# A third bank for layer 0's turned blocks, earlier mix copies and norm at the expert handover, an own bank for batch 1's logits

## The chip, the cores and the metric

The kernel runs on one core of a Trainium2 chip. The metric is the device time of one execution in microseconds (us), as a median of several runs. Beside it one execution was taken with the hardware profiler; all times of single instructions come from that one.

## The reference, cut to what matters

Two layers, each a gated cross attention and a gated feed-forward, on x of 2 batches x 256 tokens x 128:

```python
x = x + tanh(g_xattn[0]) * xattn0(layernorm(x), ctx, ctx)   # 16 heads of 8, ctx 2 x 512 x 128, mask
x = x + tanh(g_ffn[0])   * ffn0(layernorm(x))               # Hadamard, 4 bit activations, ternary weight
x = x + tanh(g_xattn[1]) * xattn1(layernorm(x), ctx, ctx)   # 16 heads of 64, mask per batch
x = x + tanh(g_ffn[1])   * moe(layernorm(x))
# attention: scores = q k / sqrt(d); softmax over 512 keys; out = probs v; out @ Wo.T + bo
# moe: softmax of 32 logits, the 4 largest with a capacity per expert, silu(x W1) * (x W3) @ W2,
#      all 32 experts of 64, summed with the gates, plus one shared expert of 128
```

## The kernel before

**Units and blocks.** An attention is cut into units: one head (layer 1) or one head of 8 (layer 0) with 128 queries against 512 keys. 64 units are layer 0's, 64 layer 1's (`TOTAL` = 128). Eight units in layer 0, four in layer 1, make a `Block` (0 to 7, and 8 to 15). Every engine runs the same written-out order of slots t from -6 on, and waits on semaphores alone.

**A unit's way.** TensorE computes scores (`scores`, L1299, in slot t for unit t+6, two score banks). VectorE masks them and takes the maximum (`mask_max`, L913, unit t+5), ScalarE takes the exponential (L729, unit t+4; it waits until the turn of six units before has freed the row buffer), VectorE the reciprocal of the sum (L922, t+3), GpSimd normalises (L586, t+3). TensorE turns the 128 x 512 block with four transposes (`turn`, L1323, unit t) into one of two `turn_bank` (banks 2 and 3), and VectorE (even units) or ScalarE (odd units and some listed ones) copies it to `probsT` (`copy_turned`, L929 and L737) in slot t+1. The turn of unit u waits for the copy of unit u-2.

**A block's end.** `mix` (L1329) multiplies all turned blocks with the values, in slot end+2 in layer 0 and end+3 in layer 1, the very last in end+1. Within a slot TensorE goes scores, jobs, mix, output projection, turn. ScalarE copies the mix (`mix_copy`, L741) in slot `copy_at`, and TensorE projects out (`project_out`, L1352) in slot `out_at` into `y_bank` (bank 7), in layer 0 once per batch. `Block` sets these slots (L81 to L83).

**Jobs.** Projections, layer norms' transposes, values and the small matmuls of feed-forward and router are "jobs" (`make_plan`, L115), placed by hand in slots and alternating over two `job_banks` (banks 5 and 6); a job waits for its bank's release by the job before it there. DMAs go through SP's queue, in the plan's order.

**Handover to the experts.** From slot 127 (`EXPERTS_AT`) the expert phase runs in halves n = 0 to 33 (17 for each batch; half p of batch b). A step e has two halves: TensorE computes `up` for W1 (even p) and W3 (odd p, six matmuls each), then `down` of the step three before. ScalarE does silu (L857), VectorE `multiply` (L1149) and `hidden` (L1162, with the gates that SP loads by DMA), ScalarE the high half of hidden (`high_hid`, L837), GpSimd its low half (`low_hid`, L630). The hidden of batch 1's steps (9, 10, ...) need batch 1's gates. In the halves of batch 0 stand still: the last attention slots (`attend(127 + p)`), layer 1's add, norm and router of batch 1 (`LATE_JOBS` L107 and `LATE_ROUTER` L108 give the halves), and weight splits on GpSimd (`WEIGHTS_LATER`, L166). Batch 1's last norm is turned, its logits computed, their maximum and exponentials taken, four experts selected, ranked, and the gates turned (`turn_gate`), written by DMA and loaded again. All these late jobs share bank 6. ScalarE takes a late job one half after TensorE, ahead of that half's silu.

## Time and profile before

| | |
|---|---|
| median of 3 runs | 278.34 us (277.91 to 278.48) |
| profiled execution | 278.08 us, its span 276.3 us |
| busy: TensorE / VectorE / ScalarE / GpSimd | 254.2 / 211.6 / 190.9 / 181.0 us |
| mean granted TensorE clock | 0.994 |
| layer 0's slots | about 16 to 90 us, its last turns to 103 us |
| layer 1's slots | to about 225 us |
| experts | 225.6 to 274 us |

A busy share is a mean over stages; the stretches and single waits in them say more. The idle time that a row gives in brackets is that of the row's engine just before it, with what released it.

### The profile page before, as it was taken

What the parts mean: (1) busy time and instruction counts of PE and PEld (TensorE: products, weight loads), DVE (VectorE), ACT (ScalarE), POOL (GpSimd) and SP (SyncE); (2) the same over time, 40 slices, a digit from 0 to 9 for tenths busy, and PEclk for the clock granted to TensorE, in tenths of its full rate; (3) what the DMA queues carried; (4) which work ended last, traced back from release to release, by engine and by line L of the source; (5) the groups of instructions that cost most, each with busy time, mean ns of one, the idle gap of its engine ahead of it and who ended that gap; (6) DMA issues with size and microseconds to landing.
All of it is one profiled execution on the core that took longest, in us unless ns stands there. A gap on an engine that the chain in (4) does not pass through costs nothing. (4 is left out here: it accounts for less than half of the span.)

```text
span 276.3 us, 6695 instructions
## 1 busy us (share of the span) xinstructions
PE 254.2 (92%) x1903; PEld 201.0 (73%) x1903; DVE 211.6 (77%) x654; ACT 190.9 (69%) x454; POOL 181.0 (65%) x271
## 2 busy tenths in 40 slices
PE   7897999999778998989999999999979989799994
PEld 5565766676547786778777788877757767799993
DVE  3999889889959795889677877787797524685683
ACT  3488779888769785857776776776866563656462
POOL 7367999675888675745743685348757794916380
PEclk9999999999999999999999999999999999889999
DMA  6558375100023675635484767676441131301540
GB/s 197 213 165 283 130 266 140 54 2 4 1 66 71 133 153 117 135 88 121 118 217 114 185 165 180 175 180 174 120 97 34 51 108 38 105 13 36 181 115 19
DMA packets 25987, 32.91 MB, mean 119 GB/s; under 512 B 4000, under 2 KB 18144, under 8 KB 25824
## 3 DMA queue, kind: packets, MB, share of 16 engines
q1 hardware_dynamic: 25520, 32.27, 43.5%
q8 instruction: 16, 0.26, 0.4%
q10 hardware_dynamic: 432, 0.22, 0.3%
q14 instruction: 19, 0.16, 0.2%
HBM read 14.32 MB, written 3.47 MB: 64 GB/s over the span
## 5 line engine op out<-in xcount | busy, mean ns | idle before, releaser
L586 POOL TENSOR_SCALAR probs<-probs,rsum 128x512 f32<-128x512 f32 x128 | 87.9, 693 | 59.0 <-DVE rsum L922 58.3
L729 ACT ACTIVATE probs<-masked,neg_max 128x512 f32<-128x512 f32 x128 | 91.8, 718 | 12.7 <-DVE neg_max L913 9.1
L1196 PE MATMUL bank<-ident,probs 128*128 128x128 f32 x512 | 78.5, 276 | 4.0 <-DVE probsT L929 2.5
L1196 PEld LDWEIGHTS bank<-ident,probs 128*128 128x128 f32 x512 | 58.5, 141 | 21.2 <-issue 11.2
L913 DVE CUSTOM_DVE_ANT_0 masked<-bank,mask 128x512 f32<-128x512 f32 x64 | 43.8, 684 | 16.4 <-PE bank L1321 16.0
L737 ACT ACTIVATE probsT<-bank 128x512 f32<-128x512 f32 x74 | 43.4, 587 | 16.5 <-PE bank L1196 16.5
L1348 PE MATMUL bank<-probsT,val 128*32 128x256 f32 (+1 forms) x512 | 46.6, 384 | 0.9 <-ACT mixT L747 0.9
L929 DVE COPY probsT<-bank 128x512 f32<-128x512 f32 x54 | 36.7, 680 | 12.5 <-PE bank L1196 12.3
L913 DVE CUSTOM_DVE_ANT_0 masked<-bank,shared 128x512 f32<-128x512 f32 x64 | 43.3, 676 | 0.4 <-PE bank L1314 0.3
L1348 PEld LDWEIGHTS bank<-probsT,val 128*32 128x32 f32 (+1 forms) x512 | 24.7, 123 | 19.0 <-issue 5.9
L1314 PE MATMUL bank<-parts 128*128 128x512 f32 x64 | 31.3, 489 | 4.4 <-DVE neg_max L913 4.4
L1320 PE MATMUL bank<-k_high,q 128*128 128x512 f32 x64 | 30.5, 477 | 1.4 <-DMA q<-q_split 1.1
L630 POOL TENSOR_TENSOR q<-masked,q 128x512 fp32r<-128x512 f32 (+1 forms) x16 | 19.9, 1258 | 17.0 <-ACT q L837 16.9
L1321 PE MATMUL bank<-k_both,q 128*128 128x512 f32 x64 | 25.2, 394 | 0.0
L729 ACT ACTIVATION_READ_ACCUMULATOR probs<-masked,neg_max 128x1 f32 x128 | 24.6, 192 | 0.0
L1149 DVE TENSOR_TENSOR bank<-bank,probsT 128x512 f32<-128x512 f32 x16 | 11.1, 696 | 13.2 <-PE bank L1203 11.6
L922 DVE RECIPROCAL rsum<-sums 128x1 f32<-128x1 f32 x128 | 20.0, 157 | 0.7 <-ACT probs L729 0.7
L857 ACT ACTIVATE probsT<-bank 128x512 f32<-128x512 f32 (+1 forms) x18 | 10.3, 572 | 14.6 <-PE bank L1203 10.4
L1314 PEld LDWEIGHTS bank<-parts 128*128 128x128 f32 x64 | 12.0, 188 | 9.3 <-DVE neg_max L913 6.7
L777 ACT ACTIVATE k_high<-bank,cols 128x512 fp32r<-128x512 f32 x16 | 11.0, 689 | 8.8 <-PE bank L1203 8.8
L986 DVE SCALAR_TENSOR_TENSOR k_low<-bank,cols,k_high 128x512 fp32r<-128x512 f32 x16 | 12.0, 748 | 6.3 <-ACT k_high L777 6.3
L837 ACT ACTIVATE q<-masked 128x512 fp32r<-128x512 f32 (+1 forms) x18 | 10.7, 603 | 4.3 <-DVE masked L1162 3.3
(238 smaller groups left out, 526.9 us busy)
## 6 DMA issues: line engine op xcount, KB each, us to landing
k_both<-k_low SPq DMA_DIRECT2D x32, 128.0 KB, 2.9
k_both<-k_high SPq DMA_DIRECT2D x32, 128.0 KB, 2.8
q<-q_split SPq DMA_DIRECT2D x32, 128.0 KB, 2.4
probsT<-staged_gate SPq DMA_DIRECT2D x32, 128.0 KB, 2.9
q<-q_split SPq DMA_DIRECT2D x32, 64.0 KB, 2.0
parts<-staged_k SPq DMA_DIRECT2D x7, 256.0 KB, 2.7
w_flat<-in_w SPq DMA_DIRECT2D x1, 1536.0 KB, 7.8
staged_k<-k_high SPq DMA_DIRECT2D x2, 512.0 KB, 3.1
```

What stands on the lines that cost most here:

```text
L586: pool.tensor_scalar(p, p, rsum[:, u % NCOL:u % NCOL + 1], 1.0, ALU.mult, ALU.mult).then_inc(normed, 1)
L630: pool.tensor_tensor(hid_low[:, e % RING, 0:cols], hidT[:, e % RING, 0:cols], hid_high[:, e % RING, 0:cols].bitcast(F32), ALU.subtract).th ...
L729: act.activation(probs[:, u % NP, :], masked[:, u % NS, :], ACT.Exp, scale=-1.0, bias=neg_max[:, c:c + 1], accum_out=sums[:, c:c + 1]).the ...
L737: act.activation(probsT[:, k.m % 2, h, :, qt * P:qt * P + P], turn_bank[u % 2][:, :].rearrange("p (k q) -> p k q", q=P), ACT.Copy).then_in ...
L913: dve.tensor_tensor_reduce(out=masked[:, u % NS, :], in0=score_bank[u % 2][:, :], in1=mask, scale=-float(k.depth) ** -0.5, scalar=3.0e38, ...
L922: dve.reciprocal(rsum[:, c:c + 1], sums[:, c:c + 1]).then_inc(recipped, 1)
L929: dve.tensor_copy(probsT[:, k.m % 2, h, :, qt * P:qt * P + P], turn_bank[u % 2][:, :].rearrange("p (k q) -> p k q", q=P)).then_inc(copied[ ...
L1196: ins = pe.transpose(dst[0:rows, t * P:t * P + P], src, ident[:, :])
L1314: pe.matmul(dst, q0[:, k.m % 4, h, q], k0[:, k.m % 4, :], start=True, stop=True).then_inc(scored, 1)
L1320: pe.matmul(dst, q1_high[:, s, h, q], k1_high[:, s, :], start=True, stop=False)
L1321: pe.matmul(dst, q1_both[:, s, h, q], k1_both[:, s, h, :], start=False, stop=True).then_inc(scored, 1)
L1348: ins = pe.matmul(mix_bank[w * h:w * h + w, 0:SQ], v[:, i, w * h:w * h + w], probsT[:, k.m % 2, h, i, :], start=(first and i == 0), stop=( ...
```

## The change

Four things are changed. (1) Layer 0's turned blocks go round three banks: 2, 3 and 7, with semaphores `copied0`; a turn waits for the copy three units back. Bank 7 was the output projection's, so layer 0's projection becomes a job `out` in a job bank, in the same slot. Layer 1 keeps two banks; its first two turns wait for layer 0's last copies in their banks. (2) The last two blocks' mix copies and projections are one slot earlier, and ScalarE takes the last attention slots two at a time, ahead of the silu. (3) Batch 1's last add, statistics and norm are one half earlier; GpSimd takes its rstd ahead of two weight splits; ScalarE and VectorE take the norm's turned block in the half in which it is turned. (4) Batch 1's logits get bank 7 and wait for ScalarE's copy of the norm only; rank and turned gates move one half later (13 to 14, 15 to 16), the router's last step two (13 to 15).

```diff
-        self.copy_at = self.mix_at + (2 if layer == 1 and not last else 1)
-        self.out_at = self.copy_at + 1
+        late = layer == 1 and b == B - 1 and g >= self.groups - 2
+        self.copy_at = self.mix_at + (2 if layer == 1 and not late else 1)
+        self.out_at = self.copy_at + (0 if last else 1)
...
-LATE_JOBS = {"ln": 7, "logits": 8, "rank": 13, "turn_gate": 15}
-LATE_ROUTER = {4: (0, 1), 6: (3,), 9: (6,), 10: (8, 9, 10), 13: (12,)}
+LATE_JOBS = {"ln": 7, "logits": 8, "rank": 14, "turn_gate": 16}
+LATE_ROUTER = {3: (0, 1), 5: (3,), 9: (6,), 10: (8, 9, 10), 15: (12,)}
...
+    for k in (BLOCKS[3], BLOCKS[7]):
+        plan.setdefault(k.out_at, []).append(("out", k.b))
...
-        i = 1 if j in last else number[j] % 2
+        i = 2 if j == ("logits", 1) else 1 if j in last else number[j] % 2
...
+def turn_home(u):
+
+    return u % 3 if u < L1_AT else u % 2
+
+
+def copies_before(i, u):
+
+    return (u - i + 2) // 3
...
-        job_banks = bank[5:7]
+        turn_bank0 = [bank[2], bank[3], bank[7]]
+        job_banks = bank[5:8]
...
             for e in range(2 * STEPS):
+                if e == 1:
+                    rstd_of(3, 1)
                 for n in WEIGHTS_LATER.get(e, ()):
                     split_weights(n)
-                if e == 1:
-                    rstd_of(3, 1)
                 low_hid(e)
...
-                    if b == 0:
+                    if b == 0 and p % 2 == 0:
+
                         attend(EXPERTS_AT + p)
+                        attend(EXPERTS_AT + p + 1)
                     for j in AFTER.get(n - 1, ()):
-                        job(j)
+                        if j != ("ln", 3, 1):
+                            job(j)
                     if p % 2 == 0:
                         wide = 2 * SQ if p < PAIRS else SQ
                         act.wait_ge(u_ready, e + 1)
                         if e >= 2:
                             act.wait_ge(hid_ready, e - 1)
                         act.activation(silu[:, e % 2, 0:wide], u_bank[e % 2][:, 0:wide], ACT.Silu).then_inc(silu_ready, 1)
+                        if n + 1 == LATE_JOBS["ln"]:
+                            job(("ln", 3, 1))
...
-                    for j in AFTER.get(n - 1, ()):
-                        job(j)
+                    for j in AFTER.get(n, ()) + AFTER.get(n - 1, ()):
+                        if (j in AFTER.get(n, ())) == (j == ("ln", 3, 1)):
+                            job(j)
...
+                elif name == "out":
+                    pe.wait_ge(mix_copied, j[1] + 1)
+                    for t in range(NQ):
+                        ins = pe.matmul(job_bank[:, t * P:t * P + P], mixT[:, (j[1] + 1) % 2, t * P:t * P + P], w0T[:, 3, :],
+                                        start=True, stop=True)
...
                 elif name == "logits":
                     pe.wait_ge(ld["wg"], 16)
-                    pe.wait_ge(*freed(("ln", 3, j[1])))
+                    pe.wait_ge(half_done, 2 * j[1] + 1)
+                    if j[1]:
+                        pe.wait_ge(y_used, 2)
...
             def turn(u):
                 pe.wait_ge(normed, u + 1)
-                if u >= 2:
-                    pe.wait_ge(copied[u % 2], u // 2)
-                turn_tiles(turn_bank[u % 2], [probs[:, u % NP, i * P:i * P + P] for i in range(NK)]).then_inc(turned, 1)
+                i = turn_home(u)
+                if u < L1_AT:
+                    if u >= 3:
+                        pe.wait_ge(copied0[i], u // 3)
+                elif u < L1_AT + 2:
+                    pe.wait_ge(copied0[i], copies_before(i, L1_AT))
+                else:
+                    pe.wait_ge(copied[i], (u - L1_AT) // 2)
...
-                for i in range(2):
-                    pe.wait_ge(copied[i], k.end // 2)
+                if k.layer:
+                    for i in range(2):
+                        pe.wait_ge(copied[i], (k.end - L1_AT) // 2)
+                else:
+                    for i in range(3):
+                        pe.wait_ge(copied0[i], copies_before(i, k.end))
```

## Rows read from the trace of the kernel before

**Rows 1.** Windows: us, then busy us (instructions) of PE, PEld, DVE, ACT, POOL, PEclk, DMA

```profile
10.00:90.00 80.00, 70.54 (x551) 50.20 (x551) 71.54 (x255) 65.52 (x167) 62.45 (x97) 1.00 0.37 116
90.00:218.00 128.00, 124.22 (x921) 98.71 (x922) 100.90 (x313) 91.47 (x225) 78.87 (x123) 1.00 0.56 136
...
240.00:244.00 4.00, 4.00 (x23) 4.00 (x23) 2.06 (x7) 3.41 (x7) 1.60 (x2) 0.58 0.25 66
244.00:268.00 24.00, 24.00 (x207) 23.66 (x206) 17.41 (x36) 13.10 (x26) 13.35 (x11) 1.00 0.33 96
```

**Rows 2.** Waits from 10 to 90 us: us in total, times, longest

```profile
DVE probsT L929 <- PE bank L1196: 5.8, 5, 1.6
...
PE bank L1196 <- DVE probsT L929: 2.5, 9, 0.6
```

**Rows 3.** Timeline, DVE and PE around one mix: start, us, engine, line

```profile
46.46 0.67 DVE L913 CUSTOM_DVE_ANT_0 masked<-bank,shared 128x512 f32<-128x512 f32 x1
...
47.21 0.48 PE L1314 MATMUL bank<-parts 128*128 128x512 f32 x1
...
47.62 1.94 PE L1348 MATMUL bank<-probsT,val 128*32 128x256 f32 x32
...
50.18 0.69 DVE L929 COPY probsT<-bank 128x512 f32<-128x512 f32 x1 [1.03 <-PE bank L1196]
```

**Rows 4.** Timeline, PE and ACT between layer 0 and layer 1

```profile
89.92 0.63 PE L1196 MATMUL bank<-ident,probs 128*128 128x128 f32 x4 [0.36 <-ACT probsT L737]
...
101.42 0.58 ACT L737 ACTIVATE probsT<-bank 128x512 f32<-128x512 f32 x1
...
101.55 0.60 PE L1196 MATMUL bank<-ident,probs 128*128 128x128 f32 x4
...
104.54 0.47 PE L1320 MATMUL bank<-k_high,q 128*128 128x512 f32 x1 [1.13 <-DMA q<-q_split]
```

**Rows 5.** Timeline, ACT, PE and DVE at the handover to the experts

```profile
223.31 1.95 PE L1348 MATMUL bank<-probsT,val 128*64 128x256 f32 x16
...
227.56 0.48 ACT L747 ACTIVATE mixT<-bank,cols 128x256 f32<-128x256 f32 x1
...
228.19 1.95 PE L1348 MATMUL bank<-probsT,val 128*64 128x256 f32 x16 [0.93 <-ACT mixT L747]
...
232.61 0.71 PE L1361 MATMUL bank<-w_out,mixT 128*128 128x128 f32 x4 [0.41 <-ACT mixT L747]
...
233.65 0.48 DVE L902 SCALAR_TENSOR_TENSOR x_sb<-bank,tanh_g,x_sb 128x256 f32<-128x256 f32 x1
...
237.97 0.41 PE L1196 MATMUL bank<-ident,xn 128*128 128x128 f32 x2 [1.09 <-DVE xn L893]
...
239.69 0.77 PE L1283 MATMUL bank<-wg,xnT 128*128 128x32 f32 x4 [0.60 <-DVE x_low L959]
```

**Rows 6.** Timeline, DVE, ACT and POOL in batch 1's logits and selection

```profile
240.49 0.23 DVE L1072 TENSOR_REDUCE lg<-bank 128x2 f32<-128x64 f32 x1 [0.95 <-PE bank L1283]
...
242.54 0.20 ACT L801 ACTIVATION_READ_ACCUMULATOR small<-bank,lg 128x1 f32 x1
...
243.40 0.16 DVE L1077 RECIPROCAL lr<-ls 128x2 f32<-128x2 f32 x1
...
245.26 1.29 POOL L630 TENSOR_TENSOR q<-masked,q 128x512 fp32r<-128x512 f32 x1 [3.66 <-ACT q L837]
...
245.40 1.23 DVE L1090 TENSOR_TENSOR small<-small,room 128x64 f32<-128x64 f32 x1
...
247.18 0.19 DVE L1093 CAST sel_b<-small 128x64 bf16<-128x64 f32 x1
```

**Rows 7.** Timeline, ACT and DVE from the turned gates to their first use

```profile
251.11 0.36 ACT L805 ACTIVATE xq<-bank 32x256 f32<-32x256 f32 x1
...
251.96 0.63 ACT L837 ACTIVATE q<-masked 128x512 fp32r<-128x512 f32 x1 [0.23 <-DVE masked L1162]
...
257.12 0.69 DVE L1162 TENSOR_TENSOR masked<-bank,probsT 128x512 f32<-128x512 f32 x1 [0.90 <-DMA probsT<-staged_gate]
```

More of the change, by code:

```diff
@@ L144, in make_plan @@
     last = [j for o in after for j in after[o]]
-    place, count = {}, [0, 0]
+    place, count = {}, [0, 0, 0]
     for j in order:
-        i = 1 if j in last else number[j] % 2
+        i = 2 if j == ("logits", 1) else 1 if j in last else number[j] % 2
         place[j] = (i, count[i])
@@ L154, in make_plan @@
             highs[j] = count
+    after = {o: tuple(js) for o, js in after.items()}
     return before, plan, after, number, place, highs
@@ L370, in build @@
         copied = [sem("copied0"), sem("copied1")]
+        copied0 = [sem(f"copied0_{i}") for i in range(3)]
         mixed = sem("mixed")
@@ L736, in copy_turned @@
                     act.wait_ge(mixed, k.m - 1)
+                i = turn_home(u)
                 act.activation(probsT[:, k.m % 2, h, :, qt * P:qt * P + P],
-                               turn_bank[u % 2][:, :].rearrange("p (k q) -> p k q", q=P),
-                               ACT.Copy).then_inc(copied[u % 2], 1)
+                               (turn_bank if k.layer else turn_bank0)[i][:, :].rearrange("p (k q) -> p k q", q=P),
+                               ACT.Copy).then_inc((copied if k.layer else copied0)[i], 1)
             def mix_copy(k):
@@ L743, in mix_copy @@
                 act.wait_ge(mixed, k.m + 1)
-                if n >= 3:
-                    act.wait_ge(projected_out, n - 2)
+                if n in (3, 4):
+                    act.wait_ge(job_done, NUMBER["out", n - 3] + 1)
+                elif n > 4:
+                    act.wait_ge(projected_out, n - 4)
                 bias = bv1[:, k.g:k.g + 1] if k.layer else bv0[:, 0:1]
@@ L751, in job @@
                 name, n = j[0], NUMBER[j]
-                if name in ("v0", "v1", "ffn", "rank", "rotate"):
+                if name in ("v0", "v1", "ffn", "rank", "rotate", "out"):
                     return
@@ L898, in add_y @@
                 x = x_sb[:, NQ * b:NQ * b + NQ, :]
-                y = (moe_bank[0][:, 0:SQ] if layer == 2 else y_bank[:, b * SQ:b * SQ + SQ]).rearrange("p (t c) -> p t c", c=P)
+                y = (job_banks[PLACE["out", b][0]][:, 0:SQ] if layer == 0 else moe_bank[0][:, 0:SQ] if layer == 2
+                     else y_bank[:, b * SQ:b * SQ + SQ]).rearrange("p (t c) -> p t c", c=P)
+                used, n = freed(("out", b)) if layer == 0 else (y_used, 2 * layer + b - 1)
                 if layer < 2:
@@ L902, in add_y @@
                 dve.scalar_tensor_tensor(out=x, in0=y, scalar=tanh_g[:, gate:gate + 1], in1=x,
-                                         op0=ALU.mult, op1=ALU.add).then_inc(y_used, 1)
-                dve.wait_ge(y_used, 2 * layer + b + 1)
+                                         op0=ALU.mult, op1=ALU.add).then_inc(used, 1)
+                dve.wait_ge(used, n)
             def mask_max(u):
@@ L928, in copy_turned @@
                     dve.wait_ge(mixed, k.m - 1)
+                i = turn_home(u)
                 dve.tensor_copy(probsT[:, k.m % 2, h, :, qt * P:qt * P + P],
-                                turn_bank[u % 2][:, :].rearrange("p (k q) -> p k q", q=P)).then_inc(copied[u % 2], 1)
+                                (turn_bank if k.layer else turn_bank0)[i][:, :]
+                                .rearrange("p (k q) -> p k q", q=P)).then_inc((copied if k.layer else copied0)[i], 1)
             def job(j):
@@ L1039, in feed_forward @@
                 if o == 0:
-                    dve.wait_ge(projected_out, b + 1)
+                    dve.wait_ge(job_done, NUMBER["out", b] + 1)
                     dve.wait_ge(tanh_ready, 1)
@@ L1324, in turn @@
                 pe.wait_ge(normed, u + 1)
-                if u >= 2:
-                    pe.wait_ge(copied[u % 2], u // 2)
-                turn_tiles(turn_bank[u % 2], [probs[:, u % NP, i * P:i * P + P] for i in range(NK)]).then_inc(turned, 1)
-            def mix(k):
-                for i in range(2):
-                    pe.wait_ge(copied[i], k.end // 2)
+                i = turn_home(u)
+                if u < L1_AT:
[5 more added lines that the diff above has]
+                    pe.wait_ge(copied[i], (u - L1_AT) // 2)
+                turn_tiles((turn_bank0 if u < L1_AT else turn_bank)[i], [probs[:, u % NP, n * P:n * P + P] for n in range(NK)]).then_inc(turned, 1)
+            def mix(k):
+                if k.layer:
[4 more added lines that the diff above has]
+                        pe.wait_ge(copied0[i], copies_before(i, k.end))
                 if k.layer == 0:
@@ L1354, in project_out @@
                 pe.wait_ge(mix_copied, n)
-                if k.layer == 1 and k.g == 0:
+                if k.g == 0:
                     pe.wait_ge(ld["bo1"], 32)
-                if (k.layer == 0 or k.g == 0) and (k.layer or k.b):
-                    pe.wait_ge(y_used, 2 * k.layer + k.b)
+                    if k.b:
+                        pe.wait_ge(y_used, 1)
+                    else:
+                        pe.wait_ge(copied0[2], copies_before(2, L1_AT))
                 for t in range(NQ):
@@ L1361, in project_out @@
                     ins = pe.matmul(y_bank[:, c:c + P], mixT[:, n % 2, t * P:t * P + P],
-                                    w1_out[:, k.g, :] if k.layer else w0T[:, 3, :],
-                                    start=((k.layer == 0 or k.g == 0) and t == 0),
+                                    w1_out[:, k.g, :], start=(k.g == 0 and t == 0),
                                     stop=(k.g == k.groups - 1), skip_group_check=True)
@@ L1387, in attend @@
                         mix(k)
-                    if t == k.out_at and (k.layer or k.g == 3):
+                    if t == k.out_at and k.layer:
                         project_out(k)
@@ L1417, in down @@
                 if d == 0 and b:
-                    pe.wait_ge(y_used, 4)
+                    pe.wait_ge(*freed(("logits", 1)))
                 if b == 0:
```

17 lines of the change are left out of this document (9 added, 8 removed).

## The prediction

> **What bounds the kernel now.** I read the windows first, then the waits in each, then the order of single instructions at the waits. Three stretches have three limits. In layer 0 (10 to 90 us) VectorE is busy 71.5 of 80 us; in layer 1 (90 to 218 us) TensorE is busy 124 of 128 us; from 244 to 268 us TensorE has no gap, 207 matmuls in 24.00 us, so 0.116 us each [rows 1]. In the matmul-bound stretches a gain is passed on to the end and nothing of it is lost; between layer 1 and the last stretch stand the gaps of the handover, with a clock at 0.58 from 240 to 244 us [rows 1]. So two places can pay: VectorE's stalls in layer 0, and the handover.
>
> **Third bank for layer 0's turned blocks.** What it takes away is TensorE's wait for the copy two units back. That wait is 2.5 us in nine places, but VectorE, the bound, waits for turned blocks only 5.8 us in five places [rows 2]. Is it the same wait? [rows 3] show one of the five. VectorE ends the masking of unit E+6 at 47.13 (46.46 plus 0.67); the scores of unit E+8, which need its score bank, start at 47.21; the mix of 32 matmuls follows at 47.62 and takes 1.94, and the turn is behind it; the copy waits for that turn until 50.18, 1.03 us. No copy is late there: TensorE is held by the two score banks and by the mix's own 1.9 us, and both stay. So the third bank is worth nothing at the mixes. Where it does count is where ScalarE or VectorE has a job in front of a copy and TensorE reaches something that VectorE needs: in the trace at 89.92, where the turn waits 0.36 us for ScalarE's copy and the first layer 1 scores stand behind it [rows 4]. I take 0.3 us for that. Bounds: nothing, and 0.8 us (0.36 and the other late turns, of 0.3 us each, if one more of them counts).
>
> Against it stand three costs. Unit 64 turns into the bank that unit 63 left, so its turn now waits for copy 63, which ScalarE starts at 101.42 and ends at 102.0 [rows 4]. The turn ran at 101.55, so it and the scores, query job and turn queued behind it move by 0.5 us. The scores of unit 72 wait 1.13 us for the queries' DMA until 104.54 [rows 4]; the DMAs in question were issued before, so the 0.5 us is covered, and shows in full if that DMA comes a microsecond earlier. The output projection as a job keeps its matmuls and its slot, at equal cost; it holds a job bank until VectorE's add one slot on, while the next job that depends on it, `turn_x`, waits for that add anyway: nothing, bound 0.3 us. Mixes wait for three semaphores, not two, eight times: nothing, bound 0.1 us each or 0.8 us in all. Layer 0 and its end together: **-0.3 us**, between -0.8 and +0.8.
>
> **Last mixes' copies.** ScalarE takes both copies of the last two blocks ahead of its silus. Now mixT of block 14 is copied at 227.56, behind silu 0 and copy 127, and the last mix starts at 228.19 after 0.93 us of waiting; the last output projection waits 0.41 us at 232.61 [rows 5]. The mix of block 14 starts at 223.31 and ends after 1.95, at 225.3 [rows 5]; the first silu's matmuls come only after it, so ScalarE can copy it before. Block 15's copy stands before silu 1, whose matmuls come after the mix anyway. What hides its 0.48 us is the six matmuls (0.7 us) between. Both waits go: -1.3 us on TensorE.
>
> **Norm in front.** VectorE adds the output projection and takes statistics in half 3, before hidden 1, and normalises in half 5, not 6; GpSimd computes rstd before two weight splits. Added waits: VectorE stands at the add until projection 15 ends, with multiply 1 behind it, whose matmuls come right after that projection, so nothing is held. The turn of the norm waits 1.09 us at 237.97 now [rows 5]. On the new order xn is there at about 235.0, by my estimate: the mix starts at 227.5 behind projection 14, so projection 15 ends at 230.8, 2.8 us before the add of now at 233.65 [rows 5]; add 0.5 us and statistics 0.9, multiply and hidden 1 at 0.69 each [rows 7], the two normalisations 1.4, with GpSimd beside them. TensorE arrives at the same time, so this wait goes too. The turn is then up to 2.9 us earlier: 0.93, 0.41, 1.09, and 0.4 us of other time around such waits.
>
> **Own bank for the logits.** They wait for ScalarE's copy alone, and no longer for VectorE's low half: the 0.60 us at 239.69 go [rows 5]. Summed, TensorE waits 3.0 us less (0.93 + 0.41 + 1.09 + 0.60). The half-speed clock, which set in after these waits, costs 4.00 x (1 - 0.58) = 1.7 us [rows 1] and I expect it to go with them. TensorE alone would gain 4.7 us.
>
> **Which wait ends last then.** Not TensorE's. Batch 1's gates come at the end of a chain: maximum of the logits, exponentials, selection, rank, turned gates, DMA out and back, and hidden 9. That one already waited for DMA until 257.12 [rows 7], some 0.1 us from holding TensorE. So I follow the chain.
> - Maximum: before it VectorE has two multiply and hidden pairs and the low half, 2 x 1.4 + 0.4 us, from 235.0: 238.3, where it was 240.49 [rows 6]: 2.2 us earlier.
> - Exponentials: from the end of the maximum (240.72) to their last read (242.74) 2.0 us, table load within; the selection started at 243.40, since VectorE was still in hidden 4 [rows 6]. Now hidden 4 is done first: ScalarE, 0.2 us late from its own high half, ends at 240.8. So 2.6 us earlier.
> - Selection: 3.9 us to the cast's end at 247.3. In it one comparison took 1.23 us; it stood from 245.40 to 246.6 beside a GpSimd subtraction from 245.26 to 246.55, and the two operations of its size between it and the cast at 247.18 fill 0.55 us together [rows 6]. So 1.0 us of the chain is that meeting, and whether it happens again depends on where GpSimd's low half of step 4 falls: by the same counting 243.2, in the midst of the last operations. I take half: 3.1 us earlier, between 2.6 and 3.6.
> - Turned gates: the job moves from half 15 to 16, so on ScalarE it goes behind the high half of step 7, not 6. That copy ran at 251.96 to 252.6, the job at 251.11 [rows 7]. So the move costs 1.5 us: 1.6 us earlier, between 1.1 and 2.1.
> - DMA: from the turned gates at 251.11 to hidden 9 at 257.12 are 6.0 us [rows 7]. That tail moves as a whole; SP has nothing else in front.
>
> TensorE comes 3.4 us earlier (4.7 less 0.5 at the rank, which it reaches a little before the selection is done, and 0.8 where down 5 waits for GpSimd) and waits at steps 12 and 13 for hidden 9 and 10. Then it is busy to the end. The end thus moves by the chain: **-1.6 us**.
>
> **Sum.** Profiled execution: 278.08 - 0.3 - 1.6 = 276.2 us. The median of the runs was 278.34, 0.26 above that execution, so 276.4 us. The forecast's own range is 275.4 to 277.6: the low end takes both bounds, the high one the larger of them alone, since the two have nothing in common.
>
> The Trainium skill (SBUF — State Buffer, Who interferes with whom) has the two engines share a port pair, and the later of a two-input VectorE instruction and a reading GpSimd instruction blocks until the first ends; the pair at 245.26 and 245.40 agrees. By that rule each of the selection's operations with two inputs can meet a low half, and two meetings instead of half a one would leave the chain 0.1 us early instead of 1.6.
>
> **Rivals.**
> - *Gates are not last* (0.10). If the chain is as fast as TensorE, because ScalarE's job finds its place sooner, the end moves by TensorE's 3.4 to 4.1 us, with the first 0.3: 274.3. For it: hidden 9's wait was only 0.90 us. Against: the job order on ScalarE is fixed.
> - *The clock falls again* (0.11). TensorE gets new waits, 0.9 us at down 5 and 0.8 to 1.0 us at steps 12 and 13, in front of the stretch that has no slack. A fall like that at 240 costs 1.7 us: 278.1. Against: two gaps, of 1.09 and 0.60 us [rows 5], stood just before that one, while TensorE's wait of 1.13 us at 104.54 [rows 4] left the clock at 1.00 [rows 1].
> - *Selection meets GpSimd twice, or the third bank costs its bound* (0.07): 278.34 - 0.3 - 0.1, or 278.34 + 0.8 - 1.6, 277.7 in the middle.
> - *The mixes' stall goes as well* (0.07). Should the turn bank be what holds TensorE there after all, 5.8 us of VectorE's stalls go, with 1.6 at the end: 271.
> - *Slower: the late turn_gate* (0.11). The chain gains only by its start; its two jobs were moved back. If the maximum isn't earlier, as GpSimd or the rstd holds the norm behind low half 0, the 1.5 us of the later place are all that is left: 278.34 + 1.5 - 0.3 = 279.5. It decides as soon as the selection starts less than 1.5 us earlier than at 243.40. The same holds if the change doesn't do what it says at the norm.
>
> **Chances.** Forecast 0.54, the rivals as given. A measurement here tells about 0.2%, 0.56 us. Faster by more than that: 0.54 + 0.10 + 0.07 and a third of the rival of 277.7, 0.73; within it the rest of that one and the clock, 0.15; slower 0.12. The range for 8 in 10 takes in the gates and the clock rival and leaves out the two outer ones: 274.2 to 278.2.
>
> **What the profile after should show.** In 10 to 90 us VectorE's waits for turned blocks still 5 to 6 us, with TensorE's for copies nearly gone; a turn near 101 waiting for ScalarE's copy. No wait at the last mix, projection, norm turn and logits; clock 1.00 at 240 us; selection from about 240.5; the turned gates' copy near 249.2; hidden 9 waiting over 2 us for DMA, and TensorE waiting at steps 12 and 13. Wrong would be: stalls at the mixes of other length, a clock fall behind 245, or a gates' copy later than 250.5.

## The result, and the profile after

The changed kernel took 279.81 us (median of 6 runs, 279.02 to 280.81) beside 278.29 us for the kernel before (6 runs): a ratio of 1.0051, 95% interval 1.0030 to 1.0073. In a second comparison it was 279.19 against 278.15 us, 1.0038 (1.0020 to 1.0055). So it is 1.0 to 1.5 us slower, where 276.4 was forecast and 274.2 to 278.2 was the range. Its profiled execution took 279.41 us with a span of 276.5 (before: 278.08 and 276.3).

The windows of the changed kernel, with the columns of [rows 1], and its waits from 10 to 90 us and from 218 to 277 us:

```profile
10.00:90.00 80.00, 69.46 (x555) 50.73 (x553) 71.55 (x252) 65.52 (x167) 62.57 (x97) 1.00 0.38 116
90.00:218.00 128.00, 124.66 (x921) 98.68 (x920) 101.42 (x315) 91.93 (x225) 79.39 (x123) 1.00 0.56 136
240.00:244.00 4.00, 3.96 (x30) 3.61 (x30) 2.63 (x13) 3.84 (x9) 1.61 (x2) 1.00 0.20 63
244.00:268.00 24.00, 20.12 (x169) 19.55 (x170) 15.66 (x26) 11.12 (x22) 12.64 (x11) 1.00 0.34 96
```

```profile
PE bank L1351 <- DVE neg_max L940: 8.9, 17, 1.3
...
DVE probsT L957 <- PE bank L1226: 5.8, 5, 1.6
...
DVE masked L1191 <- DMA probsT<-staged_gate: 3.1, 1, 3.1
...
PE bank L1231 <- DVE masked L1191: 1.8, 2, 1.5
```

Read against [rows 1 and 2]: VectorE's five waits for turned blocks in layer 0 are still 5.8 us. TensorE no longer waits for copies there but for VectorE's maxima, 8.9 us in place of these:

```profile
PE bank L1314 <- DVE neg_max L913: 4.4, 7, 1.2
```

The half-speed clock at 240 us is gone in this trace. And the stretch that had no gap, 244 to 268 us, now has 3.9 us of idle TensorE. It came early and waited 1.23 us for the selection and 0.86 for ScalarE's high half, and then 1.50 and 0.33 us for VectorE, which waited 3.1 us for the gate rows:

```profile
245.19 0.20 PE L1328 MATMUL bank<-sel_b,ones_b 128*128 128x32 bf16 x2 [1.23 <-DVE sel_b L1122]
...
257.98 0.38 PE L1231 MATMUL bank<-x_high,w_early 128*128 128x256 f32 x1 [1.50 <-DVE masked L1191]
```

The steps between layer 0 and layer 1, and the handover (TensorE and ScalarE; compare [rows 4 and 5]):

```profile
102.01 0.63 PE L1226 MATMUL bank<-ident,probs 128*128 128x128 f32 x4 [0.46 <-ACT probsT L755]
104.07 0.47 PE L1357 MATMUL bank<-k_high,q 128*128 128x512 f32 x1 [0.17 <-DVE neg_max L940]
...
225.14 0.47 ACT L767 ACTIVATE mixT<-bank,cols 128x256 f32<-128x256 f32 x1 [0.66 <-PE bank L1395]
...
227.47 1.95 PE L1395 MATMUL bank<-probsT,val 128*64 128x256 f32 x16
230.16 0.61 PE L1410 MATMUL bank<-w_out,mixT 128*128 128x128 f32 x4
235.38 0.41 PE L1226 MATMUL bank<-ident,xn 128*128 128x128 f32 x2 [0.37 <-DVE xn L918]
236.34 0.57 PE L1320 MATMUL bank<-wg,xnT 128*128 128x32 f32 x4
```

Every step of the handover is earlier than in [rows 5]: the norm's turn by 2.59 us (237.97 to 235.38), the logits by 3.35 (239.69 to 236.34). The chain of the gates goes on from there (compare [rows 6 and 7]):

```profile
238.25 0.21 DVE L1101 TENSOR_REDUCE lg<-bank 128x2 f32<-128x64 f32 x1
...
241.06 0.17 DVE L1106 RECIPROCAL lr<-ls 128x2 f32<-128x2 f32 x1 [1.21 <-ACT small L821]
...
243.59 1.23 DVE L1121 TENSOR_TENSOR small<-small 128x64 f32<-128x64 f32 x1
244.85 0.20 DVE L1122 CAST sel_b<-small 128x64 bf16<-128x64 f32 x1
...
249.36 0.38 PE L1226 MATMUL bank<-ident,small 128*32 128x128 f32 x2
...
249.97 0.63 ACT L857 ACTIVATE q<-masked 128x512 fp32r<-128x512 f32 x1 [1.20 <-DVE masked L1191]
250.50 0.36 ACT L825 ACTIVATE xq<-bank 32x256 f32<-32x256 f32 x1
...
257.23 0.69 DVE L1191 TENSOR_TENSOR masked<-bank,probsT 128x512 f32<-128x512 f32 x1 [3.13 <-DMA probsT<-staged_gate]
```

| step of the gates' chain | before | after | earlier by |
|---|---|---|---|
| maximum of the logits | 240.49 | 238.25 | 2.24 |
| selection starts | 243.40 | 241.06 | 2.34 |
| selection's cast | 247.18 | 244.85 | 2.33 |
| copy of the turned gates | 251.11 | 250.50 | 0.61 |
| tenth product (hidden 9) | 257.12 | 257.23 | -0.11 |

So the gain of 2.3 us is lost in two places: 1.7 us between cast and copy, where the two jobs were moved one half later, and 0.7 us in the transfer behind the copy, whose length had been 6.01 and is 6.73 us. From the tenth product to the end both kernels run alike (VectorE's last add at 273.57 and 273.70).

**The transfer behind the copy.** The turned gates are stored to DRAM and read back as rows. A landing is one increment of the transfer's semaphore; one issue has 16 of them, and the reader waits for the last. SP issues the loads of a step's gate rows in two halves. The loads' time from issue to landing (least, median, most, in us), first of the kernel before for its first two (issued at 253.0 and 253.6), then of the changed kernel (252.4 and 253.0):

```profile
DMA to landing us min/median/max: 2.8/3.1/3.4
```

```profile
DMA to landing us min/median/max: 2.8/3.5/4.1
```

The first half takes as long as before, the second 0.7 us longer. The view of the DMA queues of the changed kernel from 254.8 to 255.0 us (queue, kind, packets, MB, share of 16 engines' time) shows what else ran:

```profile
q1 hardware_dynamic: 35, 0.03, 57.2%
q8 instruction: 1, 0.02, 29.2%
```

One packet of 16 KB on queue 8, of the kind "instruction", started at 254.90 and took 0.93 us. Before, such a packet came at 257.40, after the rows had landed (257.00). There are 16 or 17 of them in a run, about one for each 256 instructions of TensorE's stream (4285 before, 4292 after; nearly all come 180 to 260 instructions behind a multiple of 256, by a count of TensorE's instructions in the traces). So I take them for loads of TensorE's program: where TensorE is in its program sets when they come. "Load" below means such a packet. The change made TensorE 2.5 us earlier there and the gates only 0.6, and the packet slid from behind the rows into them. The rows' two loads land in 32 parts: 31 of them had landed by 256.35, the last came at 257.11. That is the theory which the runs below test (theory A of the expectations; by theory B the rows are late for another reason).

The Trainium skill (DMA: Bandwidth & Descriptors, Queues, rings and completion order) says that a DMA engine drains one queue's packet before it takes another's; by its section on why a DMA increments its semaphore by 16 and not by 1, each of 16 engines posts its own part. One late landing of 32 beside one 0.93 us packet agrees with both; which engine carried the packet, no trace here says.

### The profile page after: what moved, and what is told of

The parts are those of the page before. It is cut to its first block and busy times, and to the rows that moved or that the text cites. A ratio compares the mean times of both kernels' runs of the same rounds, so it can differ in the third digit from the quotient of the medians.

```text
span 276.5 us, 6702 instructions
## 1 busy us (share of the span) xinstructions
PE 252.2 (91%) x1903; PEld 199.8 (72%) x1903; DVE 212.5 (77%) x654; ACT 191.3 (69%) x454; POOL 181.7 (66%) x271
## 5 line engine op out<-in xcount | busy, mean ns | idle before, releaser
L1226 PEld LDWEIGHTS bank<-ident,probs 128*128 128x128 f32 x512 | 60.0, 141 | 14.7 <-issue 7.4
```

What stands on the lines that cost most here:

```text
L1226: ins = pe.transpose(dst[0:rows, t * P:t * P + P], src, ident[:, :])
```

## The experiments

Times are medians, with the ratio to the kernel before on the same chip and its 95% interval. Kernel before: 278.15 to 278.26 us in five groups of 19 to 35 runs. "Copy" is the start of ScalarE's copy of the turned gates, "tail" the time from it to the tenth product.

### Which part loses, and what lies behind the gates

**The changed kernel again.**

> The changed kernel once more, for a second trace of it. Theory A, the end is set by the chain of the gates (turned gates, store, loads, the tenth product) and the transfers' length differs from run to run: the median is again near 279.8 and where this execution is longer than the first (span 276.5), the extra time lies between the gates' load and the product behind it, and every stretch before 250 us has the same length within 0.2 us. Theory B, the three banks cost something in layer 0: the extra time is there before 218 us. Theory C, the extra time lies outside the span.

279.19 us, 1.0038 (1.0020 to 1.0055). The tail was 6.92 us. This execution was 0.3 us late by 84 us and waited 0.72 us for the queries' transfer at 91 us; a like wait (0.63) stands in the trace of the next kernel, which costs nothing.

**The three banks alone** (all of part 1 of the change, nothing of 2 to 4).

> The kernel before with the three banks for layer 0 and the out projection as a job, and nothing of the handover. Theory A: 278.3 within 0.4, as before. Theory B: 279.5 to 280 and the runs scatter by 1.5 us or more, as the changed kernel's do. By the prediction this part is worth -0.3 us (278.0).

278.14 us, 0.9997 (0.9978 to 1.0016): nothing, as the prediction's bounds allowed.

**The handover alone** (parts 2 to 4, two banks).

> The kernel before with the handover's parts (last mixes' copies, norm in front, own bank for the logits, the later jobs) and the two banks of before. Theory A: 279.8, the whole loss and the scatter. Theory B: 276.7 to 278.0, what the prediction gave this part. Theory C (both parts add instructions that are fetched): 279.

278.91 us, 1.0036 (1.0014 to 1.0059), tail 6.83 us. The loss is the handover's.

**Without the gates' chain, after.** Edit (the second batch is weighted with the first one's gates):

```diff
-                                 staged_gate[b, 2 * d:2 * d + 2, h, :].partition_broadcast(HID)).then_inc(gate_loaded[n % GATE_SLOTS], 16)
+                                 staged_gate[0, 2 * d:2 * d + 2, h, :].partition_broadcast(HID)).then_inc(gate_loaded[n % GATE_SLOTS], 16)
...
             for b in range(B):
-                sp.wait_ge(*freed(("turn_gate", b)))
-                sp.dma_start(staged_gate[b].rearrange("p h t -> (p h) t"), gateT[b]).then_inc(gate_staged, 16)
-                sp.wait_ge(gate_staged, 16 * (b + 1))
+                if b == 0:
+                    sp.wait_ge(*freed(("turn_gate", b)))
+                    sp.dma_start(staged_gate[b].rearrange("p h t -> (p h) t"), gateT[b]).then_inc(gate_staged, 16)
+                    sp.wait_ge(gate_staged, 16 * (b + 1))
                 for d in range(QUADS):
                     load_gates(b, d)
+            sp.wait_ge(*freed(("turn_gate", 1)))
+            sp.dma_start(staged_gate[1].rearrange("p h t -> (p h) t"), gateT[1]).then_inc(gate_staged, 16)
```

> The changed kernel, but the second batch's gate rows are loaded from the first batch's stored gates, as soon as their slots are free, and the second batch's gates are stored behind them; so the second batch is weighted with wrong gates, and no product waits for its turned gates. Theory A: the waits of 3.1 us (VectorE for the load) and of 1.8 and 2.2 us (TensorE) go; 276 to 277, and the scatter falls to that of before (under 1 us). Theory B or C: the scatter of 1.8 us stays, and the time is 277.5 to 278.5.

277.00 us, 0.9946 (0.9926 to 0.9966). TensorE has no gap behind 250 us, but still 2.1 us before it, at the selection:

```profile
240.00:250.00 10.00, 7.91 (x69) 7.41 (x68) 8.54 (x23) 5.89 (x14) 4.66 (x4) 1.00 0.26 89
250.00:268.00 18.00, 18.00 (x154) 17.96 (x154) 11.63 (x20) 10.73 (x22) 10.98 (x9) 1.00 0.29 89
```

**Without the gates' chain, before.** The same edit.

> The kernel before with the second batch's gate rows loaded from the first batch's stored gates ahead of time (so the second batch is weighted with wrong gates). It gives the time of before without the gates' chain. If the chain and TensorE end together in before, as its waits say (VectorE waited 0.90 us for the rows, TensorE was never idle from 250 to 268): 278.0 within 0.4, and the changed kernel's 277.0 under the same edit is a gain of 1.0 on TensorE's side, where the prediction had 4.7. If the chain of the gates alone sets the end of before: 276.5 to 277.3, and the change gained nothing on TensorE's side that can be seen.

277.95 us, 0.9993 (0.9979 to 1.0006). So before, gates and TensorE end together, and the change's gain on TensorE's side is 277.95 - 277.00 = 1.0 us. The changed kernel is 2.2 us above its own TensorE; those are the gates'.

### Moving TensorE's program load

**48 instructions more on TensorE**, in layer 0, where it waits for VectorE anyway, on the changed kernel and on the one before:

```diff
                 if 0 <= t + LEAD < TOTAL:
                     scores(t + LEAD)
+                if 12 <= t < 36:
+                    for done, count in ((late_ready, 1), (ld["ident"], 16), (ld["w00"], 16), (ld["cols"], 16)):
+                        pe.wait_ge(done, count)
```

> The changed kernel with 48 instructions more on TensorE in layer 0 (waits for semaphores that have long been reached, four in each of 24 steps, of which two each are instructions of their own), where TensorE waits for VectorE anyway. TensorE's stream is loaded 16 KB at a time, once in 256 of its instructions, and the load that lay at 254.9 us (among the packets of the first gate rows: 31 of 32 packets' landings by 256.35, the last at 257.11) moves to about 252.5. Theory A, this load delays the gate rows: the last landing comes within 0.4 us of the one before it, copy of the turned gates to tenth product is 6.0 us in place of 6.7 to 6.9, and the time falls from 279.2 to 278.4. Theory B, the rows are late for another reason (order, addresses, other transfers): 6.7 to 6.9 us and 279.2 as before.

278.42 us, 1.0018 (0.9993 to 1.0043), 0.8 us under the changed kernel, which the intervals do not separate. The load moved further than meant, to 250.97, onto the gates' store. The rows then landed in one go (31st 256.76, 32nd 256.89), but the store's last part came 0.88 us behind its 15th (253.15 and 252.27). Tail 6.56 us. The lateness moved with the load from the rows to the store, which theory B excludes. The time came out at the 278.4 that was expected, but by luck: the tail was to be 6.0 us.

> The kernel before with the same 48 instructions. Its load of TensorE's stream at 257.4 us, behind the landing of the first gate rows (257.0), moves to about 255, among them. Theory A: copy to tenth product 6.7 to 6.9 us in place of 6.0, and the time rises from 278.15 to between 278.6 and 279.0. Theory B: 6.0 us and 278.15 within 0.2. If 48 more instructions cost by themselves, both this kernel and the one with the same edit on the changed kernel are slower.

277.12 us, 0.9959 (0.9944 to 0.9975): faster, where I expected a loss. Two things, by the traces. The load came at 254.73, too late for the first rows (last landing 255.07; tail 5.67), and hit the second ones (256.35, 256.94, 257.28), which nobody waits for so soon. And the load that had lain at 101.97 us moved to 95.4. Before, it lay on the stacking of a block's queries (two last landings 104.21 and 104.40, the others by 103.11), with the scores of unit 72 waiting 1.13 us behind it [rows 4]; here they land by 103.24 and the wait is gone: 1.06 us against that trace, 0.5 to 0.9 us against the other traces of before. All six traces with a load at 101.5 to 102.3 us (the three of before, the same with the gates cut, the handover alone, and the jobs back with two banks) have two last landings 0.6 to 1.1 us behind the rest there; this one and the changed kernel, with no load there, have none. So the extra instructions cost nothing that shows, and that wait of [rows 4] was the same collision.

**26 more on the changed kernel** (the same loop over 13 steps).

> The changed kernel with 26 more instructions on TensorE in layer 0, to put its stream load at 252.4 to 253.4, between the landing of the gates' store (252.3) and the first packets of their rows (253.5). Theory A (the load's place makes the tail): if it falls there, copy to tenth product 5.9 to 6.1 us and 278.2 to 278.4; if it misses and falls on the rows (from 253.5) or the store (until 252.3), 6.6 to 7.2 us and 278.5 to 279.5, with one landing late in the transfer that it fell on. Theory B: 6.7 to 6.9 us wherever it falls.

279.17 us, 1.0027 (1.0008 to 1.0045). The load did not move out of the rows: it started 0.36 us behind their first landing, and one landing was late again (256.85, then 258.08). Tail 6.84 us. That is theory A's second branch, and no test against B.

### The copy of the turned gates

**Copy ahead of `high_hid(7)`**, on the changed kernel:

```diff
-                        if j != ("ln", 3, 1):
+                        if j not in (("ln", 3, 1), ("turn_gate", 1)):
                             job(j)
...
+                        if n == LATE_JOBS["turn_gate"]:
+                            job(("turn_gate", 1))
                         for done in HIDDEN_AT.get(e - 1, ()):
```

> The changed kernel, with ScalarE's copy of the turned gates ahead of its copy high_hid(7) and not behind it. Theory A, the gates' chain sets the end: the copy starts 0.5 us earlier (250.0), every later step of the chain with it, and the time falls by 0.5 us to 278.7; if the transfer stream load then meets the rows in another way, by 0 to 0.9. Theory B (TensorE's path sets the end): no change, 279.2.

277.73 us, 0.9982 (0.9968 to 0.9997): 1.5 us under the changed kernel. Measured from matmul 540 (at 84 us, to take out how an execution began), the copy is 0.9 us earlier than the mean of the traces with the changed handover, and the tail 6.06 us. The load still began among the rows' landings, but 0.56 us behind the first (254.78, load 255.34) where the changed kernel had 0.26, and none was late (last landings 256.28 and 256.39).

**The same with 80 more instructions, and with 34.**

> The changed kernel with ScalarE's copy of the turned gates ahead of high_hid(7), and 80 instructions more on TensorE in layer 0, so that its stream is loaded near 250, ahead of both the gates' store (packets from 250.9) and their rows. Theory A: no last landing lags; copy to tenth product 5.6 to 6.0 us, time 277.0 to 277.5, 0.3 to 0.7 under the copy alone (277.73). Theory B, the gain of the copy alone was all there is: 277.7, and if 80 instructions cost by themselves: above it.

278.19 us, 1.0002 (0.9989 to 1.0016), 0.5 us more than the copy alone, where 0.3 to 0.7 less was expected; the intervals just overlap. The load lay at 251.03, on the store (15th landing 251.72, 16th 253.05). The store's time to landing, first with the copy alone, then with 80 instructions more, and its issue in the second:

```profile
DMA to landing us min/median/max: 1.5/1.5/1.5
```

```profile
DMA to landing us min/median/max: 2.8/2.8/2.8
```

```profile
250.26 0.33 SPq L571 DMA_DIRECT2D staged_gate<-xq  x1
253.07 0.57 SPq L560 DMA_DIRECT2D probsT<-staged_gate  x1
```

> The copy of the turned gates first, with 34 more instructions; store and rows are 0.7 us earlier here, so the load should fall at 251.7 to 252.7. Theory A: tail 5.8 to 6.0 us, 277.4 to 277.7, where 80 instructions gave 7.2 us and 278.19. Theory B: 278.2, as with 80 instructions, since it is their number that costs.

277.15 us, 0.9962 (0.9945 to 0.9979), tail 5.48 us: 34 instructions are faster than 80, clear of both intervals, and not slower than none, so it is not their number that costs. The load fell at 254.12, later than meant, 0.58 us behind the first rows' first landing; none of those was late, and two of the second rows were (256.05, then 256.74 and 256.94).

### The two jobs back

**Rank, turned gates and the router's last step at the halves of before** (13, 15, 13), on the changed kernel.

> The changed kernel with rank, turned gates and the router's last step at the halves that they had before (13, 15, 13 in place of 14, 16, 15). Theory A: the prediction charged one half later with 1.5 us of the gates' chain and the trace shows 1.8; the copy of the turned gates starts at 248.7 in place of 250.5, and the gate rows have landed before TensorE's stream is loaded (254.9), so 0.7 to 0.9 more is won on them: tenth product 2.4 us earlier, where TensorE (277.0 with the gates cut) becomes the bound: 277.0 (276.7 to 277.4). Theory B: the two jobs, early again, make TensorE wait for VectorE's selection, which costs what they bring: 278.5 to 279.2.

276.78 us, 0.9947 (0.9929 to 0.9965), as theory A had it. From matmul 540 the copy is 1.7 us earlier (164.8 against 166.2 to 167.1 us), the tail 5.77 us, and VectorE waits 0.66 us for the rows.

**The same with 48 more instructions.**

> Jobs back as in the run of that name, and 48 instructions more on TensorE in layer 0 (stream load near 251, between store and rows in this kernel). Theory A: the gates' chain no longer ends last, so this brings nothing over the jobs alone (within 0.3); if it does, the stream load still lay on the rows there.

277.20 us, 0.9962 (0.9941 to 0.9984), which the intervals do not separate from the jobs back alone. Its load fell at 252.64, just between store (252.27) and rows (first landing 254.42): no landing late in either, tail 5.96 us. The profiled execution had TensorE's clock at half speed for 3.4 us from 246, behind TensorE's wait of 2.14 us for the selection, as 3 of its 12 runs did (277.87 to 279.07; the others 275.18 to 277.60).

**The same with two banks.**

> The handover's parts with two banks, and rank, turned gates and the router's last step at the halves of before. If the third bank is worth nothing, as the prediction's -0.3 and the run with the banks alone (278.14) say: 276.8 within 0.3, as with three banks. If its out job and added waits cost TensorE something that the gates' chain hid: 276.3 to 276.5. If it brings something that the gates' chain hid: 277.1 to 277.4.

276.08 us, 0.9926 (0.9906 to 0.9946), of five executions; a sixth, the profiled one, took 1371 us and is left out of all this. Once more:

> The version with two banks and the jobs back once more, for a trace. 276.1 within 0.4. If the gates' chain is no longer last, VectorE's wait for the gate rows is under 0.8 us, copy to tenth product 5.6 to 6.0 us, and TensorE is never idle from 250 to 266.

276.32 us, 0.9945 (0.9923 to 0.9967): the fastest version, 2 us under before and 3 us under the changed kernel. Its chain and window:

```profile
249.20 0.36 ACT L807 ACTIVATE xq<-bank 32x256 f32<-32x256 f32 x1
...
254.67 0.69 DVE L1169 TENSOR_TENSOR masked<-bank,probsT 128x512 f32<-128x512 f32 x1 [0.35 <-DMA probsT<-staged_gate]
```

```profile
250.00:268.00 18.00, 18.00 (x155) 18.00 (x153) 11.85 (x20) 10.29 (x20) 11.67 (x10) 1.00 0.44 127
```

The load lies at 255.49, behind the rows (254.55), and TensorE is never idle. The tail is 5.47 us, a little under the 5.6 expected. Against three banks (276.78) it is 0.5 to 0.7 us less, which the intervals do not separate.

**The logits in the shared bank again**, on the changed kernel.

> The changed kernel with the second batch's logits in the shared bank again, behind VectorE's low halves. By the prediction's term, TensorE waits 0.60 us again at the logits, and the maximum, the exponentials and the selection start 0.5 us later; as VectorE's order holds the maximum back to 238.25 anyway, 0 to 0.5 us: 279.2 to 279.7.

279.72 us, 1.0050 (1.0031 to 1.0070): 0.5 us more, at the expected edge and within what the intervals leave. Tail 6.87 us, one landing late (256.16, then 257.59).

### The kernel before, and its clock

> The kernel before once more, for a trace of it in which TensorE's clock need not fall at 240 us. Theory A: without the fall TensorE is some 1.5 us further at 250, its stream load comes at 255.5 to 256 and not at 257.4, on the gate rows, one of their landings is late, and the tail is 6.5 to 7 us; so the time is not better than with the fall: 278.2. Theory B (the half clock costs before 1.7 us, as the prediction has it): 276.6 without it.

> The kernel before once more. Theory A, in an execution without the fall of the clock at 240: stream load at 255.2 to 256 on the gate rows, one landing late, tail 6.5 us or more, time 277.6 to 278.4. Theory B (the fall costs 1.7 us): 276.6. With the fall, the load comes behind the landing, the tail is 5.6 to 6.0, and the question stays open.

277.97 and 278.26 us (0.9994 and 0.9996). The first profile again had the half clock at 240, with a tail of 5.64 us. The second did not: load at 255.34, rows by 255.84 with none late, one of the second rows late (256.84, then 257.96), tail 5.81, and 277.03 us, the least of its eight. Theory A's late rows are not in it. But nor does the half clock cost anything in the medians: of 152 runs of the kernel before, the 49 with a mean clock of 0.994 or less have a median of 278.15 us, the 101 with 0.998 or more 278.27. A part of it the traces show. Without the fall TensorE comes to the rank before the selection is done and waits, in the third trace and, with 0.80 us, in the kernel before with its gates cut; the two traces with the fall have no wait of TensorE from 240 to 270:

```profile
246.55 0.20 PE L1291 MATMUL bank<-sel_b,ones_b 128*128 128x32 bf16 x2 [0.78 <-DVE sel_b L1093]
```

Measured from matmul 540, the third trace is 2.1 us ahead of the first at matmul 1680 and 1.2 us at matmul 1740. Why nothing at all is left in the medians stays open; the load on the rows was the candidate, and no trace shows it in this kernel.

### All the traces side by side

All that have the gates' chain. Times in us; "load" is the start of the packet for TensorE, "late" the last landing's distance from the one before it, in the transfer that the load fell on.

```
kernel                      load    store's last  first rows: first, 31st, last   tail   late
before                      257.40  252.96        255.25  256.62  257.00          6.01
before again                256.71  252.59        254.91  256.20  256.26          5.64
before, third               255.34  252.00        254.50  255.75  255.84          5.81   1.12 (second rows)
before + 48                 254.73  251.37        253.66  255.05  255.07          5.67   0.34 (second rows)
banks alone                 257.02  253.68        256.25  257.84  257.86          6.15
after                       254.90  252.35        254.64  256.35  257.11          6.73   0.76 (rows)
after again                 255.87  253.20        255.49  257.10  258.16          6.92   1.06 (rows)
handover alone              255.15  252.50        254.76  256.05  257.36          6.83   1.31 (rows)
no logits bank              255.35  252.68        255.00  256.16  257.59          6.87   1.43 (rows)
after + 26                  255.87  253.21        255.51  256.85  258.08          6.84   1.23 (rows)
after + 48                  250.97  253.15        255.41  256.76  256.89          6.56   0.88 (store)
copy first + 80             251.03  253.05        255.37  256.86  256.94          7.21   1.33 (store)
copy first                  255.34  252.32        254.78  256.28  256.39          6.06
copy first + 34             254.12  251.23        253.54  254.69  254.73          5.48
jobs back                   256.22  251.67        254.00  255.25  255.47          5.77
jobs back + 48              252.64  252.27        254.42  256.23  256.24          5.96
jobs back, two banks        255.49  251.05        253.44  254.44  254.55          5.47
```

Whenever the load starts 0.26 to 0.39 us behind the rows' first landing, one landing is 0.8 to 1.4 us late and the tail is 6.7 to 6.9 us; on the store, 6.6 and 7.2; otherwise 5.5 to 6.2. Less what is late, the seven tails are 5.4 to 6.0 us, like the others. Moving the load, moving the rows, or neither gives the same picture.

It is not enough that the load starts among the rows. In four traces it began 0.56 to 0.84 us behind their first landing (copy first, the same + 34, banks alone, before third) and none of them was late; in three of these a landing of the second rows came 0.4 to 1.1 us behind the one before it. The bound between 0.39 and 0.56 us is read off these traces afterwards, and five of the six runs that were to put the load at a certain place missed it. That load and late part share a DMA engine is the likely reason; it is inferred, not seen.

This also closes the sum. Measured from matmul 540, the mean over the five traces with the changed handover and the load on the rows, against the three traces of before: copy 0.2 us earlier, tail 6.84 against 5.82, tenth product 0.8 us later. The medians differ by 1.0. The one trace of before that the prediction used had its chain late by 0.8 to 1.4 us against the other two.

## Why the prediction was wrong, by its steps

- **Third bank, -0.3 us, nothing at the mixes.** Right in its readings: 5.8 us in five waits before and after, and the turn of unit 64 waits 0.46 us for ScalarE's copy (0.5 predicted). Of the 0.3 us no run shows anything: alone, the part moved nothing (278.14 against 278.15).
- **Copies, norm, logits' bank: TensorE's waits of 0.93, 0.41, 1.09 and 0.60 us go.** Right but for 0.37 us left at the norm. Matmul 1680 of 1903 starts 4.5 us earlier than before, where 4.7 were predicted for TensorE alone; against the third trace of before, which has no fall of the clock, it is 2.6 us (from matmul 540).
- **The gates end last.** Right: VectorE waits 3.1 us for their rows, and with the gates cut the changed kernel gains 2.2 us. The rival "gates are not last" was far off.
- **Half clock, 1.7 us.** It went, but was mis-sized: a stretch of one execution, which two thirds of the others do not have, and in the medians it costs nothing. Since the gates end last, the forecast did not rest on it. TensorE's own gain is 1.0 us by the cut kernels where 3.4 were expected. Their traces, both without the fall, are 3.2 us apart at matmul 1680 and 1.6 at matmul 1740: between them the changed kernel waits 2.1 us (1.24 for the selection, 0.85 for ScalarE's high half), the one before 0.80. The prediction gave those waits 0.5 and 0.8 us.
- **Maximum 2.2 and exponentials 2.6 us earlier.** They came 2.24 and 2.34 us earlier.
- **Selection 3.1 us earlier, half of the meeting with GpSimd gone.** Failed by 0.8 us. The cast came 2.33 us earlier. The low half started at 243.47, near the 243.2 that I had counted, and met the last sum before the cast (L1121, 1.23 us) where it had met a comparison before. I had given the meeting half a chance; it came in full, as it did in the other two traces of before and in the four others with the changed handover and the load on the rows, each time at one of these last operations. By the Trainium skill's rule (SBUF — State Buffer, Who interferes with whom) such a meeting was to be had at each of these operations that has two inputs; the trace agrees, with the 1.23 us.
- **Turned gates one half later, 1.5 us.** It cost 1.7, shown by the jobs put back. The copy ran 0.61 us earlier, not 1.6: with the last point, the whole of this shortfall.
- **Transfer: "that tail moves as a whole".** Failed: this step turned a small gain into a loss. The tail is not fixed: it runs beside a load tied to TensorE's place in its program, and I moved the two by different amounts, 0.6 and 2.5 us in the first pair of traces, without asking what would then meet. Against the third trace of before, whose load already lay at 255.34, the load comes 0.3 us earlier and the copy 0.5 us later (from matmul 540), which is enough to bring the one from 0.84 to 0.26 us behind the rows' first landing. It is 1.0 us longer on average.
- **Sum.** -1.6 was the forecast at the gates; the copy's gain was 0.6 in that pair of traces and 0.2 on average, the tail's loss 0.7 and 1.0. No rival had this. The slower one (279.5) came near the measured number by luck: it had the place right, the late turned gates, and the condition wrong, since the maximum was 2.2 us earlier.
- **Bounds.** Every term of the chain was taken from one execution, whose chain was late for its kind; a range from the gates' end of one trace was too narrow at the top by 1 to 1.6 us.

## What to carry to other kernels

When the chain that ends last contains a transfer, look at what else the DMA engines carry while it is in flight, program loads too, and ask how both move: a change that shifts TensorE and the chain by different amounts makes a new meeting. Do not pay for an engine that is no longer the bound with time of the chain that is: here the two jobs moved one half later cost 2.4 us of 279.2, by 1.7 us on the chain and by the load that the transfer then met. And take the length of a transfer, or of the clock's fall, from several executions before it becomes a term.

## What was unexpected in the hardware

A 16 KB load of TensorE's program (0.9 to 1.8 us, about one in 256 instructions) made one part of a transfer in flight 0.8 to 1.4 us late, when it fell on it as the table shows. SP's issuing slows beside it too. In the 19 traces (all but the one of 1371 us), 151 of SP's 4389 DMA issues took 0.9 us or more in place of about 0.6: 126 of them beside such a load, 6 beside an 8 KB packet of the same kind on queue 14, and 19 are one issue near 37 us that takes 1.24 us in every trace. The reverse does not hold: 164 of the 290 issues beside a load took less than 0.9 us. This issue of the changed kernel began as a load did (97.8 us):

```profile
97.17 0.61 SPq L527 DMA_DIRECT2D k_both<-k_low  x1
97.82 1.99 SPq L528 DMA_DIRECT2D k_both<-k_high  x1
```

Adding 48 instructions that do nothing made the kernel before 1.1 us faster; what its traces show changed is where these loads fell. And the loads do not move in step with the instructions added: 26 more left the load where it was relative to the rows, while 48 more, and 80 more in the kernel with the copy first, both put it at 251.0.
